# Cross-attention and squared-ReLU FFN on one core: two FFN weights turned by VectorE and split by GpSimd, the second tile's scores in other PSUM banks, value rows cast earlier

## The reference

```python
x = x + xattn(layernorm(x), ctx_768, Wq, Wk, Wv, Wout, bout)
x = x + ffn(layernorm(x), W_r, W_k, W_v, mu_r, mu_k)

# xattn: 8 heads of 128; b*n rows against all b*77 = 154 context rows
sim  = einsum('hid,hjd->hij', qh, kh) * 128 ** -0.5
mean = sim.mean(-1, keepdims=True)
attn = softmax((sim - mean) * 1.5 + mean)
return einsum('hij,hjd->hid', attn, vh).reshape(...) @ Wout + bout

# ffn
x_prev = concatenate([zeros, x[:, :-1]], axis=1)
xr = mu_r * x + (1 - mu_r) * x_prev
xk = mu_k * x + (1 - mu_k) * x_prev
r  = sigmoid(xr @ W_r.T)
return r * (square(relu(xk @ W_k.T)) @ W_v.T)
```

## Time and profile before

| | |
|---|---|
| median of 3 runs | 752.24 us |
| profiled execution | 752.19 us |
| its span | 750.4 us |
| TensorE busy | 741.4 us (99%) |
| VectorE busy | 511.0 us (68%) |
| ScalarE busy | 425.3 us (57%) |
| GpSimd busy | 121.3 us (16%) |
| granted TensorE clock | 1.00 throughout |

### The profile page before, as it was taken

One profiled execution on the slowest core, in us unless ns is written; L12 is line 12 of the kernel. 1 busy time (PEld: TensorE's weight loads), 2 busy tenths in 40 slices (PEclk: granted clock), 3 DMA queues, 4 the chain that ended last, 5 costly groups with the idle time before them and its releaser, 6 DMA issues.

```text
span 750.4 us, 13618 instructions
## 1 busy us (share of the span) xinstructions
PE 741.4 (99%) x3996; PEld 647.1 (86%) x3996; DVE 511.0 (68%) x1073; ACT 425.3 (57%) x1204; POOL 121.3 (16%) x279
## 2 busy tenths in 40 slices
PE   8999999989999999999999999999999999999998
PEld 7976888888888889898988989898888988888887
DVE  2667777677776766667767666777766677776662
ACT  3677557464655657464664755466475646555432
POOL 1110001212112121212102121210202121020211
PEclk9999999999999999999999999999999999999999
DMA  9933534544445444543444454444435444343301
GB/s 301 370 115 113 173 95 148 168 142 128 146 139 167 122 134 147 161 146 108 152 129 140 129 170 137 130 138 134 152 103 175 133 149 140 117 147 103 109 30 43
DMA packets 85017, 106.54 MB, mean 142 GB/s; under 512 B 9824, under 2 KB 61818, under 8 KB 84988
## 3 DMA queue, kind: packets, MB, share of 16 engines
q1 hardware_dynamic: 84148, 105.36, 44.8%
q10 hardware_dynamic: 839, 0.83, 0.4%
HBM read 58.70 MB, written 47.45 MB: 141 GB/s over the span
## 4 chain that ended last, share of the span: by engine, by line
PE 84%; DVE 5%; ACT 4%; DMA 3%; issue 2%; SPq 1%; POOL 1%; ACTq 0%; POOLq 0%; DVEq 0%
PE ffn L485 11%; PE ffn L487 11%; PE ffn L486 11%; PE scores L486 8%; PE scores L487 8%; PE scores L485 8%; PE attended L487 7%; PE attended L486 7%; PE attended L485 7%; ACT probs L772 1%; DMA wk<-in_L_xattn_Wk 1%; ACT probs L781 1%; DMA handed<-x_rows 1%; DMA x_rows<-normed 1%; PE attended L523 1%
## 5 line engine op out<-in xcount | busy, mean ns | idle before, releaser
L486 PE MATMUL scores<-A_lo,xT_hi 128*128 128x462 f32 (+1 forms) x384 | 134.6, 350 | 0.0
L485 PE MATMUL scores<-A_hi,xT_hi 128*128 128x462 f32 (+1 forms) x384 | 134.2, 349 | 0.0
L487 PE MATMUL scores<-A_hi,xT_lo 128*128 128x462 f32 (+1 forms) x384 | 134.1, 349 | 0.0
L772 ACT ACTIVATE probs<-scores,neg_max 128x154 f32<-128x154 f32 x256 | 96.4, 389 | 38.3 <-DVE neg_max L1044 37.9
L487 PE MATMUL attended<-B_hi,pT_lo 128*128 128x512 f32 x288 | 112.4, 390 | 0.0
L486 PE MATMUL attended<-B_lo,pT_hi 128*128 128x512 f32 x288 | 112.3, 390 | 0.0
L485 PE MATMUL attended<-B_hi,pT_hi 128*128 128x512 f32 x288 | 112.0, 389 | 0.0
L1044 DVE TENSOR_REDUCE neg_max<-scores 128x3 f32<-128x462 f32 (+1 forms) x96 | 54.9, 583 | 74.6 <-PE scores L487 74.5
L1316 POOL TENSOR_SCALAR var<-stats 128x1 f32<-128x1 f32 x64 | 12.2, 191 | 470.0 <-DVE stats L991 468.9
L485 PEld LDWEIGHTS scores<-A_hi,xT_hi 128*128 128x128 f32 x384 | 72.4, 189 | 7.3 <-issue 0.8
L486 PEld LDWEIGHTS scores<-A_lo,xT_hi 128*128 128x128 f32 x384 | 72.3, 188 | 5.8
(11 more groups left out here) (177 smaller groups left out, 1528.3 us busy)
## 6 DMA issues: line engine op xcount, KB each, us to landing
prob_rows<-probs SPq DMA_DIRECT2D x32, 704.0 KB, 3.4
probs_handed<-prob_rows SPq DMA_DIRECT2D x128, 176.0 KB, 3.3
x_rows<-normed SPq DMA_DIRECT2D x61, 256.0 KB, 2.1
handed<-x_rows SPq DMA_DIRECT2D x244, 64.0 KB, 1.9
x_in<-in_x SPq DMA_DIRECT2D x32, 256.0 KB, 3.5
out<-x SPq DMA_DIRECT2D x31, 256.0 KB, 2.5
wq<-in_L_xattn_Wq SPq DMA_DIRECT2D x4, 512.0 KB, 9.9
wout<-in_L_xattn_Wout SPq DMA_DIRECT2D x1, 2048.0 KB, 14.7
```

The source lines that it names most:

```text
L485: te.matmul(psum, left[0], right[0], start=first, stop=False)
L486: te.matmul(psum, left[0], right[1], start=False, stop=False)
L487: return te.matmul(psum, left[1], right[0], start=False, stop=last)
L772: last = nc.scalar.activation(probs[:, q, cols], S[b][:, (h - h0) * J:(h - h0 + 1) * J], ACT.Exp, bias=neg_max[:, h:h + 1], accum_out=row_ ...
```

## The change

W_k and W_r are no longer transposed by TensorE. SP loads each in four DMAs, one for each quarter of 32 partitions, in pieces of 512 B; VectorE turns 32x32 blocks (`weights_turn`, four transposes of 128x512 a matrix), ScalarE casts (`weights_hi`, now after tile 0's and tile 2's work), and GpSimd subtracts (`weights_lo`, four tensor_tensor of 128x512 a matrix, in place). This turn gives the channels another order, so mu is loaded in eight DMAs in that order, and `x2_norm` writes its rows unpermuted (permuted for the last tile, which TensorE turns). W_v stays as it was, with its own semaphores.

scores(1) goes to T[0..2] with its own x columns (x1T), and turn_x(1) stands before scores(0). The blocks of B go to S[0..2] and XB instead of T[0..2] and XB. ScalarE casts value rows in pairs ahead of each of tile 1's three exponentials; VectorE takes six of them after x_turn(2), maxima(1, 2) and a statistics pair.

```diff
-            load_rows(raw_w["k"], W_k, ffn_loaded["k"])
-            load_rows(raw_w["r"], W_r, ffn_loaded["r"])
+            def load_quarters(w, src):
+                rows = src.rearrange("(b i) (q k) -> q i b k", i=Q, q=4)
+                for q in range(4):
+                    sp.dma_start(raw_w[w][q * Q:(q + 1) * Q, :, :], rows[q]).then_inc(ffn_loaded[w], 16)
+
+            load_quarters("k", W_k)
+            load_quarters("r", W_r)
...
                 for w, src in (("k", mu_k), ("r", mu_r)):
-                    sp.dma_start(mu[w][:], src.rearrange("(c p) -> p c", p=P)).then_inc(mu_loaded, 16)
+                    for q in range(4):
+                        part = src[q * P:(q + 1) * P].rearrange("(k i) -> i k", i=Q)
+                        sp.dma_start(mu[w][q * Q:(q + 1) * Q, :], part).then_inc(mu_loaded, 16)
...
             def scores(t):
                 te.wait_ge(xT_ready, t + 1)
+                hi, lo = x1T if isinstance(t, int) and t == 1 else (xT_hi, xT_lo)
+                banks = score_banks(t)
                 for b, (h0, h1) in enumerate(HEAD_BANKS):
-                    if begun(t - 1):
+                    if isinstance(t, int) and t == 1:
+                        te.wait_ge(A_ready, 3 * DC)
+                        te.wait_ge(vT_ready, 3)
+                    elif isinstance(t, int) and t == 2:
+                        if b == 0:
+                            te.wait_ge(B_ready, FULL)
+                        elif b == 1:
+                            te.wait_ge(packed_ready, 1)
+                        else:
+                            te.wait_ge(packed_rows_ready, 1)
+                    elif begun(t - 1):
                         te.wait_ge(exp_done, 3 * t + b - 2)
...
-            turn_weights(range(0, 4))
+            turn_x(1)
             te.wait_ge(A_ready, 3 * DC)
             scores(0)
-            turn_x(1)
-            turn_weights(range(4, 8))
             scores(1)
             te.wait_ge(wout_loaded, 16)
+            te.wait_ge(vT_ready, 3)
             te.wait_ge(picked_ready, 1)
-            te.wait_ge(W_ready, 8)
...
-            turn_weights(range(8, 12))
+            turn_weights("v")
...
-                to = x_view(normed2) if is_last(t) else by_quarter(normed2)
-                rows = x_view(x2[slot]) if is_last(t) else in_quarters(x2[slot])
+                to = in_quarters(normed2) if is_last(t) else normed2[:]
+                rows = by_quarter(x2[slot]) if is_last(t) else x2[slot][:]
...
             x_norm(2, 2)
-            for n in range(0, 4):
-                weights_hi(n)
-            exponentials(0, 0)
-            exponentials(0, 1)
             x_hi(1)
-            exponentials(0, 2)
+            for b in range(3):
+                exponentials(0, b)
             normalise_early(0)
             pack_hi(0)
-            for n in range(4, 8):
-                weights_hi(n)
             x_norm(3, 3)
-            exponentials(1, 0)
-            exponentials(1, 1)
-            values_hi(0)
-            exponentials(1, 2)
-            for c in range(1, 3):
+            for b in range(3):
+                values_hi(2 * b)
+                values_hi(2 * b + 1)
+                exponentials(1, b)
+            for c in range(6, 8):
                 values_hi(c)
             x_hi(2)
...
             for c in range(8, FULL + 1):
                 values_hi(c)
+            normalise_early(1)
             packed_values_hi()
+            pack_hi(1)
             for i in range(3):
                 probs_hi(0, i)
+            x_norm(4, None)
+            weights_hi("k")
             for b in range(3):
                 exponentials(2, b)
             x_hi(3)
             normalise_early(2)
             pack_hi(2)
+            weights_hi("r")
             x_norm(5, None)
             x2_norm(0, 0)
...
+            def weights_turn(w, blocks):
+
+                dve.wait_ge(ffn_loaded[w], 64)
+                to = turned_w[w][:].rearrange("p k (b r i) -> p b r k i", r=4, i=Q)
+                for b in blocks:
+                    rows = raw_w[w][:, 4 * b:4 * b + 4, :].rearrange("p r (k i) -> p r k i", i=Q)
+                    v.transpose(to[:, b], rows).then_inc(W_turned, 1)
...
-            for n in range(0, 4):
-                weights_lo(n)
+            x_lo(1)
+            weights_turn("k", range(0, 2))
+            maxima(0, 0)
+            weights_turn("k", range(2, 4))
+            maxima(0, 1)
             x_statistics(3, 3, 1)
-            for b in range(3):
-                maxima(0, b)
-            x_lo(1)
+            maxima(0, 2)
+            weights_turn("r", range(0, 2))
             inverse_early(0)
             normalise_late(0)
+            maxima(1, 0)
             pack_lo(0)
-            for n in range(4, 8):
-                weights_lo(n)
+            weights_turn("r", range(2, 4))
+            maxima(1, 1)
+            x_turn(2)
+            maxima(1, 2)
             x_statistics(4, None, 1)
-            for b in range(3):
-                maxima(1, b)
-            values_lo(0)
-            x_turn(2)
+            for c in range(6):
+                values_lo(c)
             inverse_early(1)
-            values_lo(1)
+            for c in range(6, 8):
+                values_lo(c)
             normalise_late(1)
-            values_lo(2)
             x_lo(2)
-            for c in range(3, 6):
-                values_lo(c)
-            pack_lo(1)
-            for c in range(6, FULL):
-                values_lo(c)
+            values_lo(8)
             pack_values()
             probs_turn(0)
+            pack_lo(1)
             pack_values_lo()
...
+            def weights_lo(w):
+                for c in range(DC):
+                    pool.wait_ge(W_hi_ready, DC * "kr".index(w) + c + 1)
+                    gp.tensor_tensor(WT[w][1][:, c, :], turned_w[w][:, c, :], WT[w][0][:, c, :].bitcast(F32), ALU.subtract
+                                     ).then_inc(W_ready, 1)
...
             x_root(4)
-            x_root(5)
             pool.wait_ge(packed_lo_ready, 1)
             gp.memset(xn2T[:, :, 0:1], 0.0).then_inc(halo_zeroed, 1)
+            weights_lo("k")
+            x_root(5)
             x2_root(0)
+            weights_lo("r")
             x2_root(1)
```

More of the change, by code:

```diff
@@ L307, in head_columns, with score_banks @@
             return h // 2, slice((h % 2) * J, (h % 2 + 1) * J)
+        def score_banks(t):
+            return T if isinstance(t, int) and t == 1 else S
         WQ_BANKS = T + [XB]
@@ L539, in gate_rows @@
                 else:
[L540 removed]
+                    te.wait_ge(W_ready, 2 * DC)
+                    te.wait_ge(Wv_ready, DC)
                 te.wait_ge(mixed_split["r"], 2 * q + j + 1)
@@ L580, in last_value_rows, with turn_weights @@
                     last.then_inc(last_done, 1)
-            def turn_weights(chunks):
-                for n in chunks:
-                    w, c = "krv"[n // DC], n % DC
-                    te.wait_ge(ffn_loaded[w], 16)
-                    if n >= len(W_BANKS):
-                        te.wait_ge(W_ready, n - len(W_BANKS) + 1)
-                    elif n:
-                        te.wait_ge(vT_ready, n)
-                    else:
-                        te.wait_ge(A_ready, 3 * DC)
-                    if n == 2 * DC:
-                        te.wait_ge(B_ready, FULL)
-                        te.wait_ge(packed_ready, 2)
-                    to = W_BANKS[n % len(W_BANKS)]
+            def turn_weights(w):
+                te.wait_ge(ffn_loaded[w], 16)
+                te.wait_ge(exp_done, 6)
+                te.wait_ge(B_ready, FULL)
+                for c, bank in enumerate(W_BANKS):
                     for m in range(DC):
-                        last = te.transpose(to[:, m * P:(m + 1) * P], raw_w[w][:, m, c * P:(c + 1) * P], identity[:])
-                    last.then_inc(W_turned, 1)
+                        last = te.transpose(bank[:, m * P:(m + 1) * P], raw_w[w][:, m, c * P:(c + 1) * P], identity[:])
+                    last.then_inc(Wv_turned, 1)
             def step(g, s):
@@ L759, in x_hi @@
                 act_e.wait_ge(x_turned, t + 1)
-                if begun(t - 1):
+                if begun(t - 2):
                     act_e.wait_ge(scores_done, 3 * t)
-                copy(xT_hi[:], x_view(O) if turned_by_pe(t) else xT[:]).then_inc(xT_hi_ready, 1)
+                copy((x1T[0] if isinstance(t, int) and t == 1 else xT_hi)[:], x_view(O) if turned_by_pe(t) else xT[:]).then_inc(xT_hi_ready, 1)
             def exponentials(t, b):
@@ L951, in _ @@
                 probs_hi(1, i)
-            for n in range(8, 12):
-                weights_hi(n)
+            weights_hi("v")
             for b in range(3):
@@ L1131, in last_rows @@
                     v.tensor_tensor(x2[3][:, cols], gate[1][:, cols], x2[3][:, cols], ALU.add).then_inc(last_ready, 1)
[L1133 to L1141 removed]
+            def weights_turn(w, blocks):
[5 more added lines that the diff above has]
+            def weights_lo(w):
```

(8 more changed lines are left out.)

63 lines of the change are left out of this document (26 added, 37 removed).

## The result

The changed kernel takes 755.66 us, the median of 16 runs (753.49 to 759.84); the kernel before, timed beside it in 16 runs, 753.73 us (751.95 to 754.38). The ratio is 1.0032, with an interval of 1.0019 to 1.0046: slower by about 2.4 us (1.9 by the two medians), where the forecast was +0.2 us and a range that ended at +1.5. In absolute time it is 3.3 us above the forecast of 752.4; 1.5 of these are the kernel before, whose first three runs gave 752.24 and all sixteen 753.73. Medians here are over all runs and ratios over the fast ones, without one run of whole loads at 914 us (granted clock 0.754) and one of the kernel before at 1914 us.

The account below looks back on a forecast made before the run. TensorE alone bounds the kernel up to attend(0), then a chain through the other engines to 152.4; -3.5 + 3.45 + 0.25 = +0.2 us against 752.19 gave 752.4 us, with an 8-in-10 range of 749.3 to 753.7.

Parts of the forecast that it names:

- TensorE up to attend(0): TensorE from the start to attend(0): 32 transposes removed, scores(2) at 58.05 instead of 61.54, -3.5 us.
- The loads: W_k, W_r in 512 B pieces on SP: 7.3 instead of 5.3 us, hand_x(2) moved to 41.0, free for the total.
- 2.1 of clearance: Before x_turn(2): hand_x(2) down at 44.8, wanted at 46.95, so its lateness costs nothing.
- The bounds, 0 and +15.8: Limits on the loads' added time: 0, or +15.8 us if one piece is as dear as another.
- SP's 12 added issues: On SP's queue: 12 more DMA issues of 0.43 us each hide in its existing 2.5 us waits.
- The exclusion of VectorE and GpSimd: At probs_lo(1) beside GpSimd's W_r subtractions: two-SBUF-input instructions wait for each other and take turns, +3.45 us on the chain.
- +0.25 for tile 0: At probs_lo(0) beside GpSimd's W_k subtractions: maxima(2, 0) 1 us late, add_x(0)'s slack takes most, +0.25 us.
- VectorE is served first: Rival at probs_lo: VectorE goes first once it waits, +0.95 instead of +3.45, total 749.9 us; chance 0.13.
- Partial: Rival at probs_lo(1): ports are shared and both engines run slower, +2.15 us, total 751.0 us; chance 0.08.
- GpSimd keeps its turn: Rival at probs_lo(0): GpSimd is not let go before its fourth subtraction ends, +4.05 us, total 756.2 us; chance 0.08.
- The balance at 152.4: At the end of the xk_lo gap: TensorE's early gain returns as waits; the balance there is the whole change.
- pieces, not bytes: Rival on SP's loads: 3072 more pieces cost +15 us, hand_x(2) eight late, TensorE waits 7.2, end 759.6; chance 0.03.

Follow-up runs that it names:

- whole loads: The changed kernel with W_k and W_r loaded in one DMA each, 2 KB pieces to 128 partitions: 753.76 us, ratio 1.0006 to the kernel before.
- Both: The changed kernel with W_k and W_r in one DMA each and GpSimd's eight subtractions replaced by zero memsets: 750.26 us, ratio 0.9952 to the kernel before.
- fills: The changed kernel with GpSimd's eight W_k and W_r subtractions replaced by zero memsets, which read nothing: 751.11 us, ratio 0.9976 to the kernel before.
- GpSimd held back: The changed kernel with GpSimd's W_k subtractions behind VectorE's probs_lo(0), the last three of W_r behind probs_lo(1): 751.56 us, ratio 0.9986 to the kernel before.
- the last kernel: The changed kernel with loads reordered on SP and GpSimd's subtractions waiting for VectorE's probs_lo: 750.64 us, ratio 0.9969 to the kernel before.

## Why the prediction was wrong, step by step

**TensorE up to attend(0): right.** scores(0), values_out and scores(2) were forecast for 33.06, 46.8 and 58.05. After has the first two at 33.86 and 47.50, 33.0 and 46.6 without the late start; whole loads show 58.20 for the third, 57.95 without their start 0.25 us later, with the 0.8 us of wait at the end of values_out that the sum contained (0.85). Taken alone the change of TensorE is worth -3.6 us by the ratio, with 1.3 to either side; -3.5 was said.

**The loads: this step failed.** "The 512 B pieces of handed at 130 GB/s at a share of 0.45, so 289 at a full one" was taken for the whole price. It was right for the size of the pieces: those to 128 partitions went at 287 (279 to 311 in the stretches around), and put hand_x(2) 2.05 us later than whole loads did; +2.0 was forecast. What it left out is that each DMA of the change writes to 32 partitions. handed does so too, but it ran at a share of 0.45, and dividing by the share took for granted that no other limit comes before the full share; the row was extrapolated past what it had seen. In after, 170 to 201 GB/s: hand_x(2) went out at 48.26 - 0.87 = 47.4 instead of 41.0, 6.4 late against 2.1 of clearance, x_turn(2) was 3.7 late and TensorE waited 3.0. W_r was down at 42.1, 7 us later than said. The bounds, 0 and +15.8, held the true value, +8.4, but they were used as two ends and nothing between them had a chance of its own. In the sum the term for the loads was nothing; by the ratios it measured 1.8 to 2.0 us.

A smaller miss stands in the same step: SP's 12 added issues were to "hide". With whole loads hand_x(2) is still 14.1 us behind turn_x(0), and 13.9 in "Both", where before it was 13.1; no kernel isolates these 0.8 to 1.0 us, which the clearance of 2.1 covers.

The Trainium skill (SBUF — State Buffer, section "Door 1: The DMA port swizzle") had said that 32 partitions reach 8 of 16 ports, about 218 GB/s. The kernel with 2-KB pieces to 32 partitions shows 209 to 229 in the five stretches from 28 to 38, which agrees, and 147 in the one before them. By its rule the prediction priced the loads at +4.3 us and x_turn(2) at 0.2 late, and gave this no chance. It was nearer than the sum, and still short: in the kernel that ran at about the page's rate hand_x(2) came 19.8 us behind turn_x(0), 6.7 more than before. The 0.8 to 1.0 us of the whole loads and the slow first stretch are part of the rest.

A second reader of the same queue was missed: x_in(3). It stood behind both matrices, and VectorE waited 2.77 us for it at 42.59, ahead of maxima and the W_r transposes. In the forecast it appeared in the list of what is queued behind the loads and in no sum. By itself it did not set block 4's time in this execution, since VectorE waited another 1.86 us for hand_x(2) afterwards.

**The exclusion of VectorE and GpSimd: right.** Forecast: probs_lo(1) ends 6.3 us behind the start of x2_norm(0), +3.45 on the chain, and +0.25 for tile 0. After: 6.0, that is +3.2 over the 2.86 of before, of which 3.1 arrive at x2_norm(1). probs_lo(0) took 2.58 instead of 1.49, and of that little arrives: from scores(2) to x2_norm(0) it is 16.90 us in after and 16.77 with fills, 0.1. So the traces give 3.3 and the comparisons of ratios 4.1 to 4.2 (3.5 to 3.8 by the medians), with 3.7 forecast. Between x2_norm(1) and xk_lo(1) after takes 1.3 us more than before, but that stretch also varies from 0.3 less to 1.4 more in the other kernels with these collisions and from 0.1 to 0.9 more in those without; its share in the comparisons stays open. The rows of single copies did carry: one waits until the other has ended, and turns change between instructions. "VectorE is served first" would have ended 3.8 behind and "Partial" 5.0, and partial would have slowed GpSimd's second subtraction, which took its 1.29; "GpSimd keeps its turn" would have shown no VectorE subtraction done before GpSimd's fourth. None came. The Trainium skill (SBUF — State Buffer, section "Who interferes with whom") says that a VectorE instruction with two inputs in SBUF contends with a GpSimd instruction that reads SBUF, and not with one that only writes; the traces of subtractions (4.67 us) and of fills (1.50 us) agree, the fills with half a microsecond of overlap only.

**The balance at 152.4: right.** What TensorE gained by scores(2) it gave back in waits, at scores(4) (1.9 us) and at xk_lo (2.8 instead of 2.4), and with whole loads the end moved by 0.5 us.

**The sum.** -3.6 for TensorE, +4.1 for the subtractions, +1.9 for the loads: +2.4, against -3.5, +3.7 and 0. The rival that came nearest in its mechanism was "pieces, not bytes", a late hand_x(2) and a wait in block 4, at a chance of 0.03 and a price of 7.2 us of wait; its reason was wrong (as many pieces of 512 B to 128 partitions made hand_x(2) only 2.05 us later than whole loads), its consequence was right at two fifths of the size. The range ended at 753.7, 1.5 us over before, because a clearance of 2.1 us behind a price known only from a half-empty queue was treated as certain.

**What stays open.** The profile of after lost 1.7 us to the clock three times. How often that falls to a run, and what share of the 1.9 us of the loads it makes, was not separated; a kernel that delays block 4 by a known time was not tried.

## What to carry to other kernels

A rate read while the DMA engines are half idle, scaled up by their share, can be far too high: here it gave 289 GB/s and 170 to 224 came. Scale it only if the destination, partitions and pieces, has been seen under load. When a load gets slower, list everything that is queued behind it on the same queue with the time at which each is wanted, and move the ones with slack (here mu, W_v and the early tile) behind the ones without, before the load itself is made faster. Work moved to GpSimd costs VectorE time wherever both have subtractions with two SBUF inputs at once, here 3.2 us for three of VectorE's beside four of GpSimd's; two waits that keep them apart, and the new order of loads, made +2.4 us into -2.3.

## What the runs showed of the hardware that I had not expected

Pieces of 512 B and a destination of 32 partitions each slow a load: 384 to 392 GB/s with neither, 279 to 311 with pieces of 512 B, 209 to 229 with 32 partitions (and 147 in the first stretch). With both it was 170 to 201 in after and up to 224 with GpSimd held back. All this is with the DMA engines' share at 1.0 or above, so a full share says nothing of the rate.

TensorE's granted clock fell from 2.4 to 1.2 GHz late in gaps of 1.9 to 3.1 us or behind them, and stayed down for some 3.4 us, 1.7 us of work lost each time; with whole loads it was down for 6.8 us from 152.4 on, in a gap of 2.77 and behind it. It did not fall behind every such gap: before's of 2.42 us, the 2.81 of the last kernel, 2.75 with fills and 1.94 with whole loads left the clock at 1.00 in their profiled executions, and one of 1.30 did too. A gap on TensorE therefore costs its own length and sometimes 1.7 us more, once 3.4.

The slow loads were not equally slow in each execution: from turn_x(0) to the issue of hand_x(2) it was 21.5 us twice (after, and with fills) and 19.1 once (GpSimd held back) with the same eight DMAs.
